# Two-head attention units on partition halves, without stacking transfers, in a gated attention and expert kernel

## The chip, the cores and the metric

One core of one Trainium2 chip. The metric is the device time of one execution in microseconds. The change is compared with the kernel before by medians of several runs.

## The reference

Two batches of 256 tokens of width 128 pass a gated attention and a gated mixture of experts; a context of 512 rows per batch gives further keys and values.

```
k = concat(LN(x) @ Wk1, ctx @ Wk2);  v = concat(LN(x) @ Wv1, ctx @ Wv2)   # 768 keys, 8 heads of 64
attn = softmax((LN(x) @ Wq1) k^T / 8);  x = x + tanh(g0) * ((attn v) @ Wo + bo)
combine = softmax of the top 2 of 8 of (LN(x) @ gate_w + gate_b)
out = x + tanh(g1) * (sum_e combine_e * ffn_e(LN(x)) + shared_ffn(LN(x)))  # gelu, hidden 512
```

Nine feed-forward networks (8 experts and the shared one) for two batches make 18 FFN steps.

## The kernel before

Precision comes from splitting each operand into an fp16 high part and an fp16 rest. ScalarE writes the high part, VectorE the rest out of PSUM (L720 for projections), and TensorE does three matmuls (hi hi, hi lo, lo hi; `three`, L904).

*Items.* `ITEMS` lists 27 projection outputs: transposed context `tc` and rows `tx`, keys `k` of a head pair (768 columns), queries `q`, values `v` of a key tile. Each passes TensorE, ScalarE (L589), VectorE (L720). The first 18 run ahead of attention, 9 are late items inside its steps. The weights are split by ScalarE and VectorE (L557, L692), and WV2 and WO by GpSimd (L501 to L505).

*Stacking.* A head has 64 rows. To fill 128 rows, SP's queue copies k and q, high parts and rests, from `k_nat` and `q_nat` into `kab` and `qab` (`stack_k`, `stack_q`, L404 to L425). These issues stand in one queue with the loads of the FFN weights (`load_f`, L388); the ring of FFN weights has 4 slots.

*Attention.* One step per head, 16 of them. `max_scores` (L987, L988) gives rough scores of 128 queries by 768 keys, VectorE takes their maximum (L735), a transpose (L1024) and L832 make of it a shift row. `scores` (L1006, L1007) is two matmuls per tile of 128 keys: 128 stacked rows, and 66 rows (rest and shift). ScalarE does the exponential (L598) and the fp16 copy (`make_hi`, L606) on 128x768, GpSimd the rest (`prob_lo`, L521), TensorE the product with v (`values`, L1041 to L1043), VectorE the division (L740, L745). The lags between these are 2, 3 and 4 steps. PSUM: banks 0 and 1 for maxima, 2 to 5 for scores, 6 for values, 7 for the rest.

*Tail.* When a batch's heads are done, stages run at fixed steps (`TAIL0`, `tail_of`): two transposes with a split (O0, O1), the product with Wo and row statistics (WO), normalised rows xn (X: power on GpSimd L538, VectorE L686, transpose L1065), router logits (GATE, exponential on GpSimd L542), the combination weights (COMB: VectorE L761 to L771, transpose L1076), bias (B2).

*FFN.* In FFN step k: h = W1 x (12 matmuls, L906 to L908), gelu (L642), fp16 cast on VectorE (L852), rest on GpSimd (L549), y = W2 h two steps later (24 matmuls of 128 columns), accumulation (L884). gelu(k) waits for the rest of step k-2. The weights of networks 0 to 2 are split by GpSimd ahead of attention (`split_early`, L489, L491, L493); those of 3 to 8 by ScalarE (L649) and VectorE (L892) in FFN steps 0 to 5. The first FFN step is step 18, so COMB of batch 0 (step 19) comes behind h(1).

The order on each engine is the program's: each engine runs through the steps and executes its parts of a step in the order written.

Of the kernel before, what the change touches and what calls it, by code (L numbers as in the profile page):

```python
# [14 lines left out]
F32 = mybir.dt.float32  # L15
F16 = mybir.dt.float16
# [4 lines left out]
P = 128  # L21
# [19 lines left out]
RING = 4  # L41
# [7 lines left out]
SHIFT_PAIR, = unpack("<f", pack("<ee", SHIFT_ROW, SHIFT_ROW))  # L49
# [6 lines left out]
ST_LAG = 2  # L56
HI_LAG = 3
PV_LAG = 4
FFN0 = NH + ST_LAG
# [3 lines left out]

TAIL0 = [HEADS + PV_LAG, NH + PV_LAG + 1]
BIAS_STEP = 10
EARLY = 3
FSPLIT0 = 15
# [4 lines left out]
def late_items(i, q):  # L72

    if i >= len(LATE_PLAN):
        return range(0)
    counts = [c for step in LATE_PLAN for c in step]
    n = NI - LATE + sum(counts[:2 * i + q])
    return range(n, n + counts[2 * i + q])


def place(h):

    return h % 2 * PAIRS + h // 2


def tail_of(i):

    return [(b, i - TAIL0[b]) for b in range(B) if i - TAIL0[b] in TAIL_STAGES]


def plan_items():

    items = [("tc", 0), ("tx", 0)]
    for p in range(PAIRS):
        items += [("k", 0, p), ("q", p)]
    items += [("v", 0, 0), ("tc", 1)]
    items += [("v", 0, t) for t in range(1, KT)]  # L100
    items += [("v", 1, t) for t in range(KT - LAST_V)]
    items += [("k", 1, p) for p in range(PAIRS)]
    items += [("v", 1, t) for t in range(KT - LAST_V, KT)]
    return items


LAST_V = 2
ITEMS = plan_items()
NI = len(ITEMS)
WARM_START, WARM_LAYERNORM, WARM_STEP = 14, 9, 8  # L110


LATE_PLAN = [(2, 2), (2, 1), (0, 1), (0, 1)]
LATE_SLOT = [1, 2, 3, 1, 2, 1, 2, 3, 3]
LATE = len(LATE_SLOT)

SLOT = [(n - (NI - LATE)) % 4 for n in range(NI - LATE)] + LATE_SLOT


def before(n, slot):  # L120

    return max([m + 1 for m in range(n) if SLOT[m] == slot], default=0)

SPLIT_BEFORE = {1: [WK2, WK1], 2: [WQ], 5: [WV2], 8: [WV1], 10: [WO]}
SPLIT_ORDER = [w for n in sorted(SPLIT_BEFORE) for w in SPLIT_BEFORE[n]]
# [5 lines left out]
GROUPS = [[(0, 1), (1, PAIRS)], [(0, 2), (2, PAIRS)]]  # L133


def group_of(b, p):

    return max(p0 for p0, _ in GROUPS[b] if p0 <= p)


LO_LAST = NH - 1


def lo_tiles(j):

    return 3 if j < LO_LAST else 0


def pool_lo(j, g):

    return 2 * j + g + 1 - max(0, j - LO_LAST + (g == 1)) if j >= 0 else 0
# [22 lines left out]
def shifts_before(n):  # L174

    return sum(1 for u, m in MISC.items() if m < n and u[0] == "shift")


def plan_misc():

    uses = []
    for i in range(STEPS):
        if 1 <= i <= NH:
            uses.append(("shift", i - 1))
        if i == BIAS_STEP:
            uses.append(("b1", 0))
        for b, s in tail_of(i):
            uses.append((s, b))
    return {u: n for n, u in enumerate(uses)}
# [5 lines left out]
def block_kernel(nc, x, ctx_in, g_xattn, g_ffn, Wq1, Wk1, Wv1, Wk2, Wv2, Wo, bo,  # L195
                 gate_w, gate_b, w1, b1, w2, b2, ws1, bs1, ws2, bs2, out):
    stack = ExitStack()
    with stack:
# [23 lines left out]
        kab = sb("kab", [P, 2, HEADS, KEYS], F16)  # L222
        k_a = kab[:, 0]
# [135 lines left out]
        def item_out(n):  # L359

            kind = ITEMS[n][0]
            return span(2 * SLOT[n], KEYS if kind == "k" else 512)
# [833 lines left out]
```

## Time and profile before

| | us |
|---|---|
| median of 3 runs (172.03 to 174.6) | 172.52 |
| profiled execution | 172.02 |
| its span, first to last instruction | 169.7 |
| PE / DVE / ACT / POOL busy | 139.7 / 131.2 / 109.6 / 126.8 |
| mean granted TensorE clock | 0.988 |

PE is TensorE, DVE VectorE, ACT ScalarE, POOL GpSimd. The time is read as the span plus the 2.3 us around it. Busy PE counts pipelined matmuls: one lasts 0.27 us and the next starts 0.11 us after it.

### The profile page before, as it was taken

Reading aid. Unit: us, or ns where it says so; the run is one execution under the profiler, and the core shown is the slowest. Engines: PE = TensorE matmul, PEld = TensorE weight load, DVE = VectorE, ACT = ScalarE, POOL = GpSimd, SP = SyncE. Lnnn points to the kernel's source line nnn. Section 1 sums busy time; section 2 is a strip of 40 time slices with the busy share of each in tenths; the row PEclk is TensorE's granted clock in tenths of the full one; section 3 lists DMA queues with packets and bytes.
Section 4 is the critical chain, followed back from the end, with each engine's and each line's share of the span. In section 5 each row is a group of like instructions: output and inputs, shape, how many; then the busy total and the mean of one; then the engine's idle time right before and its main releaser. Section 6 shows DMA issues by size and latency. Waiting matters only on the chain.

```text
span 169.7 us, 4332 instructions
## 1 busy us (share of the span) xinstructions
PE 139.7 (82%) x1724; PEld 111.5 (66%) x1724; DVE 131.2 (77%) x255; ACT 109.6 (65%) x182; POOL 126.8 (75%) x90
## 2 busy tenths in 40 slices
PE   7789588558699989999998892979866995999953
PEld 4435234335478768787787792869856994999952
DVE  1779999667667868768869689989999889454691
ACT  3369583329969979899968998569523462555600
POOL 7609999919999999989777955596557585868750
PEclk9999999999999999999999999999996999999999
DMA  4598699990004800995000000340000000100000
GB/s 136 184 315 211 196 238 242 220 251 14 6 0 85 198 1 16 217 233 191 4 4 0 4 0 0 108 144 6 2 0 0 4 0 4 31 0 4 0 0 31
DMA packets 12925, 13.99 MB, mean 82 GB/s; under 512 B 1470, under 2 KB 9579, under 8 KB 12907
## 3 DMA queue, kind: packets, MB, share of 16 engines
q1 hardware_dynamic: 12906, 13.73, 30.4%
q8 instruction: 13, 0.21, 0.6%
q14 instruction: 6, 0.04, 0.1%
HBM read 7.18 MB, written 0.26 MB: 44 GB/s over the span
## 4 chain that ended last, share of the span: by engine, by line
PE 32%; DVE 28%; POOL 10%; ACT 9%; DMA 8%; SPq 6%; issue 5%; DVEq 0%; ACTq 0%
PE banks L906 5%; DVE kab L852 5%; PE banks L908 5%; PE banks L907 5%; POOL kab L549 4%; ACT kab L642 4%; DVE v_lo L720 3%; DMA kab<-k_nat 3%; DVE nmax L735 3%; PE banks L1006 3%; PE banks L1007 3%; PE banks L987 3%; DMA ring<-in_L_ffn_w_dram 3%; SPq L425 2%; DVE gtop L763 2%
## 5 line engine op out<-in xcount | busy, mean ns | idle before, releaser
L549 POOL TENSOR_TENSOR kab<-kab 128x1024 f16<-128x1024 f32 (+1 forms) x18 | 41.1, 2283 | 17.3 <-DVE kab L852 17.3
L521 POOL TENSOR_TENSOR p_lo<-prob,p_hi 128x768 f16<-128x768 f32 x31 | 50.3, 1642 | 3.1 <-ACT p_hi L606 2.6
L642 ACT ACTIVATE kab<-banks,b1T 128x256 f32<-128x256 f32 x72 | 28.2, 478 | 24.3 <-PE banks L908 15.9
L735 DVE TENSOR_REDUCE nmax<-banks 128x1 f32<-128x768 f32 x32 | 30.5, 954 | 12.5 <-PE banks L988 12.5
L598 ACT ACTIVATE prob<-banks 128x768 f32<-128x768 f32 x32 | 25.8, 805 | 9.1 <-PE banks L1007 8.1
L906 PE MATMUL banks<-wf,kab 128*128 128x128 f16 x144 | 26.2, 224 | 5.8 <-POOL kab L549 4.5
L606 ACT ACTIVATE p_hi<-prob 128x768 f16<-128x768 f32 x32 | 27.0, 843 | 1.0
L852 DVE CAST kab<-kab 128x1024 f16<-128x1024 f32 (+1 forms) x19 | 19.5, 1031 | 9.8 <-ACT kab L642 9.8
L908 PE MATMUL banks<-wf,kab 128*128 128x128 f16 x144 | 26.2, 224 | 0.0
L907 PE MATMUL banks<-wf,kab 128*128 128x128 f16 x144 | 26.2, 224 | 0.0
L1006 PE MATMUL banks<-qab,kab 128*128 128x256 f16 x96 | 23.0, 273 | 0.7 <-DVE qab L832 0.7
L1007 PE MATMUL banks<-qab,kab 66*128 66x256 f16 x96 | 23.1, 273 | 0.0
L1041 PE MATMUL banks<-v_hi,p_hi 128*128 128x65 f16 x192 | 20.6, 194 | 2.0 <-POOL p_lo L521 2.0
L1043 PE MATMUL banks<-v_hi,p_lo 128*128 128x65 f16 x192 | 20.6, 194 | 0.0
L1042 PE MATMUL banks<-v_lo,p_hi 128*128 128x64 f16 x192 | 20.5, 193 | 0.0
L1041 PEld LDWEIGHTS banks<-v_hi,p_hi 128*128 128x128 f16 x192 | 17.8, 98 | 2.9 <-POOL p_lo L521 1.2
L906 PE MATMUL banks<-x2h,wf 128*128 128x256 f16 x72 | 19.6, 273 | 0.0
L908 PE MATMUL banks<-x2h,wf 128*128 128x256 f16 x72 | 19.6, 273 | 0.0
L907 PE MATMUL banks<-x2h,wf 128*128 128x256 f16 x72 | 19.6, 272 | 0.0
L906 PEld LDWEIGHTS banks<-wf,kab 128*128 128x128 f16 x144 | 14.5, 100 | 6.9 <-POOL kab L549 5.2
L1042 PEld LDWEIGHTS banks<-v_lo,p_hi 128*128 128x128 f16 x192 | 17.6, 98 | 0.3
L1043 PEld LDWEIGHTS banks<-v_hi,p_lo 128*128 128x128 f16 x192 | 17.6, 97 | 0.0
(144 smaller groups left out, 340.3 us busy)
## 6 DMA issues: line engine op xcount, KB each, us to landing
ring<-in_L_ffn_w_dram SPq DMA_DIRECT2D x16, 256.0 KB, 4.1
kab<-k_nat SPq DMA_DIRECT2D x4, 384.0 KB, 4.4
kab<-k_nat SPq DMA_DIRECT2D x6, 192.0 KB, 4.4
kab<-k_nat SPq DMA_DIRECT2D x2, 576.0 KB, 7.2
qab<-qo SPq DMA_DIRECT2D x2, 384.0 KB, 6.2
kab<-k_nat SPq DMA_DIRECT2D x2, 288.0 KB, 7.8
prob<-in_ctx_dram SPq DMA_DIRECT2D x2, 256.0 KB, 5.4
ring<-in_L_xattn_Wk_dram SPq DMA_DIRECT2D x2, 256.0 KB, 3.9
```

Of the source, the lines that this page charges most:

```text
L521: nc.gpsimd.tensor_tensor(p_lo[:, j % 3, dst, :], prob(j, g)[:, 0:n, :], p_hi[:, j % 3, dst, :], ALU.subtract).then_inc(pl_done, 1)
L549: nc.gpsimd.tensor_tensor(hid_lo[:, k % HB, cols], hid[:, k % 2, cols], hid_hi[:, k % HB, cols], ALU.subtract).then_inc(hl_done, 1)
L642: nc.scalar.activation(hid[:, k % 2, c * T1:(c + 1) * T1], span(2 * (k % 2), HC * T1)[:, c * T1:(c + 1) * T1], ACT.Gelu, bias=b1T[:, e * H ...
L735: nc.vector.tensor_reduce(nmax[:, i, q:q + 1], span(0, KEYS), AX_X, ALU.max, negate=True).then_inc(max_done, 1)
L906: nc.tensor.matmul(dst, w[0], a[0], start=start, stop=False)
L907: nc.tensor.matmul(dst, w[0], a[1], start=False, stop=False)
L908: return nc.tensor.matmul(dst, w[1], a[0], start=False, stop=stop)
L1006: nc.tensor.matmul(dst[:, cols], k_a[:, h, keys], q_a[:, h, queries], start=True, stop=False)
L1007: last = nc.tensor.matmul(dst[:, cols], k_b[0:DH + QT, h, keys], q_b[0:DH + QT, h, queries], start=False, stop=True)
L1041: nc.tensor.matmul(o_ps[:, q, :], ph, vh, start=(t == 0), stop=False, skip_group_check=True)
L1042: nc.tensor.matmul(o_ps[:, q, 0:DH], ph, vl, start=False, stop=False, skip_group_check=True)
L1043: last = nc.tensor.matmul(o_ps[:, q, :], pl, vh, start=False, stop=(t == KT - 1), skip_group_check=True)
```

## The change

The stacking copies and `kab`, `qab` go. k and q stay where the projections leave them: one head of a pair on partitions 0 to 63, the other on 64 to 127. Every attention matmul with k and q is done per half, the two halves alternating, into two PSUM banks. The unit of work is no longer one half of a head's keys but a pair of heads by two key tiles, 128x1024: 24 units (`NU`), three for each of 8 pairs, one per step. The shift row comes by a matmul of its own (ones row by shift) in both halves. Maxima are taken from the high parts alone (64 rows), in three chunks of 128x1024 per pair, four steps ahead. Score buffers: one (banks 2, 3) for units 0 to 8, then two. Four items stand ahead of the steps, the others at steps -4 to 7. The ring of FFN weights has 7 slots, so no load waits for stacking. On GpSimd only network 0 is split ahead of attention; networks 1 and 2, WO and the bias go between the units. The rest of the last unit is VectorE's. The 8 dummy matmuls in attention go. FFN is as before but starts at step 24 and keeps `hid` in the ring of exponentials; the first batch's tail starts at step 16, the second's at 27, so COMB of batch 0 (step 23) now stands before h(0).

```diff
-RING = 4
+RING = 7
-FFN0 = NH + ST_LAG
-TAIL0 = [HEADS + PV_LAG, NH + PV_LAG + 1]
+RINGP = 7
+RINGE = 3
+CHUNK0 = -(UPP + 1)
+DOUBLE0 = 9
+FFN0 = NU
+TAIL0 = [16, 27]
+def chunk_of(s):
+    p, c = divmod(s - CHUNK0, UPP)
+    return (p, c) if 0 <= p < NPAIR else None
+def shift_of(s):
+    p, r = divmod(s + 1, UPP)
+    return p if r == 0 and 0 <= p < NPAIR else None
+def values_of(s):
+    if s >= NU + 1:
+        return NH - 2 + s - (NU + 1) if s <= NU + 2 else None
+    p, r = divmod(s - (UPP + 2), UPP)
+    return 2 * p + r if p >= 0 and r < 2 and p < NPAIR - 1 else None
+PRE = [(("tc", 0), 0), (("tx", 0), 2), (("k", 0, 0), 4), (("q", 0), 6)]
+LATE = {
+    -4: [(("k", 0, 1), 2), (("q", 1), 7), (("k", 0, 2), 4), (("q", 2), 6)],
+    -3: [(("k", 0, 3), 2), (("q", 3), 7), (("v", 0, 0), 4), (("v", 0, 1), 5)],
+    -2: [(("v", 0, 2), 6), (("v", 0, 3), 7), (("v", 0, 4), 2), (("v", 0, 5), 3)],
+    -1: [(("tc", 1), 4), (("k", 1, 0), 6)],
+    0: [(("v", 1, 0), 4), (("v", 1, 1), 5)],
...
 # GpSimd
-            for j in range(1, EARLY):
-                if j == EARLY - 1:
-                    split_by_pool(WO)
-                split_early(j)
+            for i in range(STEPS):
+                if 0 <= i - 1 < LO_LAST:
+                    prob_lo(i - 1)
+                if i == 2:
+                    early_hi(1)
+                if i == 3:
+                    early_scaled(1)
+                if i == 4:
+                    early_lo(1)
+                if i == 5:
+                    add_bias()
+                if i == 6:
+                    early_hi(2)
+                if i == 7:
+                    early_scaled(2)
+                if i == 8:
+                    early_lo(2)
+                if i == 10:
+                    split_by_pool(WO)
 # ScalarE
+            def exp_unit(u):
+                act.wait_ge(score_ps, u + 1)
+                if u >= RINGE:
+                    act.wait_ge(pl_done, u - RINGE + 1)
...
+                if 0 <= i < NU:
+                    exp_unit(i)
+                for n in items[0:1]:
+                    item_of(n)
+                if 0 <= i < NU:
+                    make_hi(i)
+                for n in items[1:]:
+                    item_of(n)
...
+                    if k < 2:
+                        act.wait_ge(pl_done, NU - 2 + k)
 # VectorE
+            def part_max(p, c):
+                dve.wait_ge(max_ps, UPP * p + c + 1)
...
+                nc.vector.tensor_reduce(dst, src, AX_X, ALU.max).then_inc(part_done, 1)
 # TensorE
+            def scores(u):
+                p, third = divmod(u, UPP)
+                if score_before(u) > 0:
+                    pe.wait_ge(exp_done, score_before(u))
...
+                for n in range(KT2):
+                    for half in range(2):
+                        nc.tensor.matmul(dst[:, half, cols], k_of(p, half, 0, keys), q_of(p, half, 0, every), ...)
+                    for half in range(2):
+                        nc.tensor.matmul(dst[:, half, cols], k_of(p, half, 1, keys), q_of(p, half, 0, every), ...)
+                    for half in range(2):
+                        nc.tensor.matmul(dst[:, half, cols], k_of(p, half, 0, keys), q_of(p, half, 1, every), ...)
+                    for half in range(2):
+                        last = nc.tensor.matmul(dst[:, half, cols], ones_row[rows, :], shift[rows, p % 2, :], ...)
...
+            for i in range(CHUNK0, STEPS):
+                if shift_of(i) is not None:
+                    shift_row(shift_of(i))
+                if 0 <= i < NU:
+                    scores(i)
+                if chunk_of(i) is not None:
+                    max_chunk(*chunk_of(i))
                 k = i - FFN0
                 if 0 <= k < NF:
...
+                if values_of(i) is not None:
+                    values(values_of(i))
+                for n in late_items(i):
                     item_of(n)
...
                 for b, s in tail_of(i):
                     tail(b, s)
```

## Rows read from the trace of the kernel before

**Rows 1.** The page, busy time of each engine, its share, its instructions:
```profile
PE 139.7 (82%) x1724; PEld 111.5 (66%) x1724; DVE 131.2 (77%) x255; ACT 109.6 (65%) x182; POOL 126.8 (75%) x90
```

**Rows 2.** Attention stretch: busy PE, PEld, DVE, ACT, POOL (instructions), then clock, DMA share, GB/s:
```profile
48.00:76.00 28.00, 26.90 (x425) 21.83 (x423) 21.75 (x41) 24.92 (x31) 27.16 (x18) 1.00 0.48 111
```

**Rows 3.** Timeline of POOL ahead of attention: start, us, engine, line, tiles:
```profile
22.08 0.62 POOL L512 TENSOR_SCALAR bo_sb<-bo_sb,gates 128x128 f32<-128x128 f32 x1
22.78 1.69 POOL L515 TENSOR_TENSOR x_sb<-x_sb,bo_sb 128x128 f32<-128x128 f32 x4
24.43 1.89 POOL L489 TENSOR_TENSOR wf<-ring,c_sw 128x1024 f16<-128x1024 f32 x1
...
28.37 2.13 POOL L493 TENSOR_TENSOR wf<-ring,wf 128x1024 f16<-128x1024 f32 x1
30.45 1.04 POOL L501 TENSOR_TENSOR wa<-ring,c_sw 128x512 f16<-128x512 f32 x1
...
32.69 1.16 POOL L505 TENSOR_TENSOR wa<-ring,wa 128x512 f16<-128x512 f32 x1
37.72 1.89 POOL L489 TENSOR_TENSOR wf<-ring,c_sw 128x1024 f16<-128x1024 f32 x1 [3.88 <-DMA ring<-in_L_ffn_w_dram]
```

**Rows 4.** Timeline of POOL in attention:
```profile
43.76 29.41 POOL L521 TENSOR_TENSOR p_lo<-prob,p_hi 128x768 f16<-128x768 f32 x18
```

**Rows 5.** Timeline of DVE ahead of attention:
```profile
12.24 0.68 DVE L720 SCALAR_TENSOR_TENSOR qo<-banks,qo 128x512 f16<-128x512 f32 x1
...
20.73 3.76 DVE L720 SCALAR_TENSOR_TENSOR v_lo<-banks,v_hi 128x512 f16<-128x512 f32 x6
...
24.52 0.95 DVE L735 TENSOR_REDUCE nmax<-banks 128x1 f32<-128x768 f32 x1
```

**Rows 6.** Groups by line and shape: busy us, mean ns, idle before:
```profile
L735 DVE TENSOR_REDUCE nmax<-banks 128x1 f32<-128x768 f32 x32 | 30.5, 954 | 12.5 <-PE banks L988 12.5
...
L606 ACT ACTIVATE p_hi<-prob 128x768 f16<-128x768 f32 x32 | 27.0, 843 | 1.0
...
L598 ACT ACTIVATE prob<-banks 128x768 f32<-128x768 f32 x32 | 25.8, 805 | 9.1 <-PE banks L1007 8.1
```

**Rows 7.** Timeline of PE in attention:
```profile
60.67 0.27 PE L1006 MATMUL banks<-qab,kab 128*128 128x256 f16 x1
60.78 0.27 PE L1007 MATMUL banks<-qab,kab 66*128 66x256 f16 x1
...
61.12 0.19 PE L1041 MATMUL banks<-v_hi,p_hi 128*128 128x65 f16 x1
...
61.66 0.39 PE L987 MATMUL banks<-kab,qab 128*128 128x512 f16 x1
```

**Rows 8.** Timeline of POOL around the first batch's tail:
```profile
90.06 0.73 POOL L538 TENSOR_TENSOR rstd<-vare,c_mhalf 128x2 f32<-128x2 f32 x1 [1.25 <-DVE vare L679]
90.76 6.47 POOL L521 TENSOR_TENSOR p_lo<-prob,p_hi 128x768 f16<-128x768 f32 x4
...
102.68 2.12 POOL L549 TENSOR_TENSOR kab<-kab 128x1024 f16<-128x1024 f32 x1 [2.67 <-DVE kab L852]
```

**Rows 9.** Timeline of DVE around the first batch's tail:
```profile
91.72 2.36 DVE L686 TENSOR_SCALAR xn<-acc,mv,rstd 128x128 f32<-128x128 f32 x2
...
102.91 1.91 DVE L763 TENSOR_TENSOR gtop<-gtop,gexp 128x2 f32<-128x2 f32 x1
...
105.36 0.24 DVE L771 TENSOR_SCALAR comb_s<-comb,scales 128x18 f32<-128x18 f32 x1
```

**Rows 10.** Timeline of ACT in the FFN steps:
```profile
100.31 1.57 ACT L642 ACTIVATE kab<-banks,b1T 128x256 f32<-128x256 f32 x4
...
111.93 1.57 ACT L642 ACTIVATE kab<-banks,b1T 128x256 f32<-128x256 f32 x4 [2.55 <-POOL kab L549]
...
160.06 1.57 ACT L642 ACTIVATE kab<-banks,b1T 128x256 f32<-128x256 f32 x4 [1.08 <-PE banks L908]
```

**Rows 11.** Timeline of PE at the third FFN step:
```profile
105.74 0.38 PE L1076 MATMUL banks<-ident,comb 128*9 128x128 f32 x2 [3.04 <-DVE comb_s L771]
```

More of the change, by code:

```diff
@@ L9 @@
 from math import log
-from struct import pack, unpack
 import concourse.bass as bass
@@ L53 @@
 PICKED = 3.0e38
-ST_LAG = 2
-HI_LAG = 3
-PV_LAG = 4
-FFN0 = NH + ST_LAG
+KT2 = 2
+UPP = KT // KT2
+NPAIR = B * PAIRS
+NU = NPAIR * UPP
+RINGP = 7
[3 more added lines that the diff above has]
+FFN0 = NU
 NF = B * NE
 STEPS = FFN0 + NF + 4
-TAIL0 = [HEADS + PV_LAG, NH + PV_LAG + 1]
-BIAS_STEP = 10
+TAIL0 = [16, 27]
+BIAS_STEP = 12
 EARLY = 3
-FSPLIT0 = 15
+FSPLIT0 = FFN0 - EARLY
 TAIL_O0, TAIL_O1, TAIL_WO, TAIL_X, TAIL_GATE, TAIL_COMB, TAIL_B2 = TAIL_STAGES = (0, 1, 2, 4, 5, 7, 8)
[L72 to L78, printed above, removed]
@@ L81, in place @@
[L81 to L104, printed above, removed]
@@ L107, with tail_of @@
-LAST_V = 2
-ITEMS = plan_items()
-NI = len(ITEMS)
[L110 to L127, printed above, removed]
+def tail_of(s):
+    return [(b, s - TAIL0[b]) for b in range(B) if s - TAIL0[b] in TAIL_STAGES]
@@ new lines, with late_items, banks_of, before @@
+PLACED = PRE + [it for s in sorted(LATE) for it in LATE[s]]
+ITEMS = [it for it, _ in PLACED]
+BANK = [bank for _, bank in PLACED]
+NI = len(ITEMS)
+WARM_START, WARM_LAYERNORM = 14, 9
+def late_items(s):
+    n = len(PRE) + sum(len(LATE[r]) for r in LATE if r < s)
+    return list(range(n, n + len(LATE.get(s, []))))
+def banks_of(n):
+    return {BANK[n], BANK[n] + 1} if ITEMS[n][0] == "k" else {BANK[n]}
+def before(n, banks):
+    return max([m + 1 for m in range(n) if banks_of(m) & set(banks)], default=0)
@@ L171, in hid_parts @@
     return [(0, HC // 2), (HC // 2, HC)] if k in SHARED_LO else [(0, HC)]
-def shifts_before(n):
-    return sum(1 for u, m in MISC.items() if m < n and u[0] == "shift")
 def plan_misc():
     uses = []
[L182 to L185, printed above, removed]
+    for s in range(STEPS):
+        if s == BIAS_STEP:
             uses.append(("b1", 0))
-        for b, s in tail_of(i):
-            uses.append((s, b))
+        for b, t in tail_of(s):
+            uses.append((t, b))
     return {u: n for n, u in enumerate(uses)}
@@ L361, in item_out @@
             kind = ITEMS[n][0]
-            return span(2 * SLOT[n], KEYS if kind == "k" else 512)
+            return span(BANK[n], KEYS) if kind == "k" else banks[:, BANK[n], :]
         block = stack.enter_context(nc.Block())
@@ L991, in scores, with q_of @@
[L991 to L1002 removed]
+            def q_of(p, half, hl, cols):
+                b, pp = divmod(p, PAIRS)
+                return q_nat[DH * half:DH * half + DH, hl, b, pp, cols]
@@ new lines, in scores @@
+                    for half in range(2):
+                        nc.tensor.matmul(dst[:, half, cols], k_of(p, half, 1, keys), q_of(p, half, 0, every),
+                                         start=False, stop=False)
+                    for half in range(2):
+                        nc.tensor.matmul(dst[:, half, cols], k_of(p, half, 0, keys), q_of(p, half, 1, every),
+                                         start=False, stop=False)
+                    if u == 0 and n == 0:
+                        pe.wait_ge(consts, 5)
@@ L1009, in scores @@
+                    if third == 0 and n == 0:
+                        pe.wait_ge(shift_done, p + 1)
+                    for half in range(2):
+                        rows = slice(DH * half, DH * half + DH)
+                        last = nc.tensor.matmul(dst[:, half, cols], ones_row[rows, :], shift[rows, p % 2, :],
+                                                start=False, stop=True)
                 last.then_inc(score_ps, 1)
             def bank7_free(use):
-                n = MISC[use]
```

489 lines of the change are left out of this document (212 added, 277 removed), and 6 rows, old and new, of the table LATE.

## The prediction

> **What bounds the kernel now.** I read the busy times first. No engine is full over the span: PE 82%, DVE 77%, POOL 75% [rows 1]. So I read stretches. In attention, from 48 to 76 us, POOL works 27.2 of 28 us, PE 26.9 and ACT 24.9 [rows 2]. Three engines are about equal there. The reader should see that less work on one of them gains nothing unless the others follow.
>
> Then I read POOL alone, because it has no second engine to share with. Ahead of attention it waits 3.88 us for FFN weights whose load stood behind the stacking copies. It then splits network 2 from 37.72 on [rows 3], and its first p_lo starts at 43.76. Eighteen of them follow without a gap: 29.41 us, 1.634 us per 128x768 [rows 4]. The first gelu starts at 100.31 [rows 10], and 18 FFN steps and the end take the other 69.4 us. The steady distance of two gelus late in FFN is 1.57 + 1.08 = 2.65 us. Early steps take longer, 111.93 - 100.31 = 11.6 us for three [rows 10], mostly because PE waits for the router's combination weights of batch 0: they end at 105.36 + 0.24 = 105.6 [rows 9], after 3.04 us of PE waiting [rows 11].
>
> **What the change does to POOL.** p_lo becomes 23 pieces of 128x1024. The same kind of subtraction (f16 from f32 and f16) takes 2.12 us at that size [rows 8]; scaling 1.634 by 4/3 gives 2.18 [rows 4]. I take 2.12: 23 x 2.12 = 48.8 us, against 31 x 1.634 = 50.7 before. Work that stood ahead of attention now stands between units. The split of one network is 28.37 + 2.13 - 24.43 = 6.07 us, two are 12.1. The bias is 24.43 - 22.08, 2.4. WO is 32.69 + 1.16 - 30.45, 3.4 [rows 3]. Row powers and gate exponential are two short operations of 0.73, 1.5 [rows 8]. Sum: 48.8 + 12.1 + 2.4 + 3.4 + 1.5 = 68.2 us from the first p_lo to the last. Before, 17.9 us of this were done by 43.76, largely while POOL would otherwise have been idle; now POOL has nothing to do after network 0's split ends at 22.1.
>
> **When attention starts.** Stacking goes: no wait for DMAs, and FFN loads no longer stand behind them in SP's queue. The start now hangs on DVE. q of pair 0 is ready at 12.24 + 0.68 = 12.9; from there to 24.5 DVE ran 14 items and one weight split, 11.6 us [rows 5]. Two of these 14 (0.60 each, 3.76/6 by the row) now come later: 10.4. In between come three chunk maxima. At 768 columns one is 0.954 [rows 6], by size at most 1.27, and I take 1.2 because part is fixed: 3.6. The joining maximum and the shift add 0.7. Shift ready: 12.9 + 10.4 + 3.6 + 0.7 = 27.6. Then PE's chunk of pair 1 (0.45), its maximum 1.2, the context rest 0.6, k of batch 1 (1.0 by nine matmul slots of 0.11), scores 1.1: 31.95. The exponential of 128x1024 is 0.805 x 4/3 = 1.07 at most, the copy 0.843 x 4/3 = 1.12 [rows 6]; a v item of 0.6 stands between. First p_lo: about 34.5, with 32 to 36 as ends. That is 9 us earlier than now, and it is where the change earns.
>
> **POOL's chain.** Unit 1 is late by 1.2 us, since two v items and one k item stand on ACT before its copy. After that ACT needs 2.2 us per unit and its items, POOL 4.1 in steps 2 to 8, so POOL falls behind, up to the three buffers of exponentials. p_lo(18) ends at 34.5 + 1.2 + 19 x 2.12 + 12.1 + 2.4 + 3.4 = 93.9. The single score buffer costs nothing here: exponential, scores and latency are 2.4 us, and POOL's splits hide them up to unit 8. If POOL did not cover it, it would cost 9 x 0.3 = 3 us.
>
> **A new chain at the first batch's tail.** POOL's power comes behind p_lo(18): rstd at 94.6. Then DVE makes two xn tiles. In the trace these two, started at 91.72, took 2.36 us together, ending at 94.08 [rows 9], where POOL's second p_lo ended (90.76 + 2 x 1.62 = 94.0) [rows 8]. Such a DVE operation between SBUF tiles ends when POOL's running instruction does; the other case is 102.91 + 1.91 = 104.82 against 102.68 + 2.12 = 104.80 [rows 8, 9]. With units of 2.12 that gives xn at 94.6 + 4.2 = 98.8. PE waits for xn at the end of step 20, and behind it stand scores(21). Transposes 0.5, scores and latency 1.1, exponential 1.07, copy 1.12: p_lo(21) starts at 102.6, while POOL has been empty since 98.8. It ends at 104.7, the gate exponential at 105.4. p_lo(22) ends at 107.5, and L763 ends with it. The rest of the combination weights takes 105.6 - 104.8 = 0.8: ready at 108.3.
>
> **FFN after it.** Before, h(0) and h(1) ran ahead of COMB. Now COMB of batch 0 is in step 23 and PE, in order, waits for it before h(0). So all FFN steps start behind 108.3, gelu(0) at 109.6. DVE's list from there to the second cast: three normalisations (0.45 each), the last unit's rest 1.25, combT 0.4, bias 0.5, one weight split 1.2, two casts 0.7, and two waits for values, 0.9 and 1.1: 8.1. POOL's rest of step 1 is 2.1, so gelu(3) starts at 118.5 against 111.93 now [rows 10]. Behind gelu(3) both kernels have the same lists at the same distances: 57.8 us. Span 176.3, with the 2.3 us around it 178.6. That is 6.6 us over the profiled execution of 172.02 and 3.5% over the median 172.52.
>
> **TensorE.** Per pair, scores now are 48 matmuls of 64 rows and 256 columns. A matmul slot of 256 columns is 0.11 us, also where only 66 rows are used [rows 7]. If the two halves overlap fully, a unit is 8 slots, 0.88 us, and attention costs PE what it does now less half of the maxima, 5 us in all. If they don't overlap, it is 16 slots, 1.76. No row shows two disjoint halves. The 66-row row is the nearest, but it has a 128-row neighbour with which it could share nothing, so it doesn't decide; I take the lower end because each half has its own rows and its own PSUM bank, and keep both. With the lower end PE has 0.88 + 0.22 + 0.73 (values: 18 in 0.54 us, two thirds of 72) = 1.85 us per unit, below POOL's 2.12. The three matmuls of L906 to L908 are untouched.
>
> The Trainium skill, TensorEngine Tiling (Array Packing), section Tiling Modes, says that 64-row tiles work independently, but also that a change of tiling mode drains the array. By the first half of that PE stays at 1.85 per unit; by the second each step would pay for a change to 64 rows and one back. No row here shows what a drain costs.
>
> **Rivals.**
> *The halves don't overlap.* From unit 11 on PE then needs 1.76 + 0.3 + 0.73 = 2.8 us per unit, over POOL's 2.12. scores(11) can start at 69 (POOL's p_lo(8)), thirteen units and 3 us of tail end at 108.4, some 4.5 us later than in my chain; part was waiting anyway, leaving 3 us: 181.5. For it: nothing in the trace shows an overlap. Against: separate rows and banks. The change then doesn't do what its form is for.
> *No empty POOL at the tail.* If DVE gets its two xn in between POOL's units, POOL isn't starved (3.7 us back) and the router is ready earlier: 174.5, the same as before. For it: it needs only that POOL be less than a unit behind when the row powers are due, as now, where it waited 1.25 us for them [rows 8]. Against: POOL's sum, and the two rows named.
> *Faster: early FFN steps smooth.* The twelve first steps take 3.9 us each where 2.65 is steady [rows 10], an excess of 15 us, because DVE then carries the router of batch 0, weight splits and the second tail. The router's chain is now out of it, and values end before step 3. If each of these steps takes at most 3.1 us, 9.6 us come back: 169.0, and this decides faster. At the steady cadence it would be 164. Against: six weight splits and the second tail stay where they are relative to FFN.
>
> **How the numbers follow.** POOL and the tail chain as forecast: 0.50, 178.5, own range 175.5 to 181.5. No empty POOL: 0.18. No overlap: 0.17. Smooth FFN: 0.15. A measurement of this kernel tells about 2% from no change, so faster is below 169.1 and slower above 176.0. Faster 0.15; within 2% 0.27 (the second rival and the lower edge of the forecast); slower 0.58. Range 169 to 184: the unknown costs are start of attention (2 us each way), overlap (3 up), FFN pace.
>
> **What would show it.** p_lo(0) near 34.5, POOL's p_lo and splits without gaps from about 41 to 98, then a gap of some 4 us before p_lo(21). PE waiting for xn, then for the combination weights, and the first gelu at 108 to 110. Scores: 8 slots of 0.11 per unit. I am wrong if the last p_lo ends before 102, if gelu(3) comes before 114, or if a unit's 16 score matmuls take 1.76 us.

## The result, and the profile after

The changed kernel takes 187.63 us (median of 4 runs, 187.52 to 189.5) against 173.56 us for the kernel before in the same comparison. The ratio is 1.087, 95% interval 1.073 to 1.100: slower. I had forecast 178.5 us with a range of 169 to 184. The sign was right and the size was not: the loss was 14 us where I had 6, and the time lies outside the range. Some executions of either kernel are slower by a per cent or more whatever the program, and the ratios leave these out, so that a ratio can differ a little from the quotient of two medians.

The profiled execution took 187.71 us with a span of 185.9, which is 9.6 us over the 176.3 of my sum. First the busy times of the changed kernel (before: [rows 1]):

```profile
PE 145.1 (78%) x1900; PEld 109.4 (59%) x1900; DVE 130.5 (70%) x247; ACT 106.9 (57%) x166; POOL 119.9 (65%) x84
```

POOL, DVE and ACT have less to do than before, PE 5.4 us more, and the span is 16.2 us longer. So it is hardly work that was added; engines wait. Where they wait is read best from POOL, whose timeline I had forecast (start, us, engine, line, tiles, and in brackets the idle time just before with what ended it):

```profile
37.40 2.13 POOL L497 TENSOR_TENSOR p_lo<-prob,p_hi 128x1024 f16<-128x1024 f32 x1 [15.80 <-ACT p_hi L590]
40.53 2.13 POOL L497 TENSOR_TENSOR p_lo<-prob,p_hi 128x1024 f16<-128x1024 f32 x1 [1.01 <-ACT p_hi L590]
...
76.60 16.73 POOL L497 TENSOR_TENSOR p_lo<-prob,p_hi 128x1024 f16<-128x1024 f32 x8
94.18 2.13 POOL L497 TENSOR_TENSOR p_lo<-prob,p_hi 128x1024 f16<-128x1024 f32 x1 [0.85 <-ACT p_hi L590]
99.77 0.73 POOL L524 TENSOR_TENSOR rstd<-vare,c_mhalf 128x2 f32<-128x2 f32 x1 [3.46 <-DVE vare L660]
100.47 4.20 POOL L497 TENSOR_TENSOR p_lo<-prob,p_hi 128x1024 f16<-128x1024 f32 x2
109.61 2.12 POOL L497 TENSOR_TENSOR p_lo<-prob,p_hi 128x1024 f16<-128x1024 f32 x1 [4.94 <-ACT p_hi L590]
```

From 40.53 to 93.3 POOL has no gap, as forecast, and a unit takes 2.1 us. Then come the gaps: 3.46 us for the row statistics, which I had not foreseen, and 4.94 us for the next p_hi, where I had 3.8. In [rows 8] the wait for the statistics was 1.25 us. The timeline of DVE at the same place says why:

```profile
96.84 1.23 DVE L722 TENSOR_REDUCE part<-banks 128x4 f32<-128x1024 f32 x1 [2.41 <-PE banks L1001]
98.10 0.16 DVE L729 TENSOR_REDUCE nmax<-part 128x4 f32<-128x8 f32 x1
98.19 0.48 DVE L794 SCALAR_TENSOR_TENSOR acc<-banks,scales,x_sb 128x256 f32<-128x256 f32 x1
...
99.52 0.17 DVE L660 TENSOR_SCALAR vare<-mv 128x2 f32<-128x2 f32 x1
...
100.53 4.22 DVE L667 TENSOR_SCALAR xn<-acc,mv,rstd 128x128 f32<-128x128 f32 x2 [0.51 <-POOL rstd L524]
...
113.73 0.24 DVE L776 TENSOR_SCALAR comb_s<-comb,scales 128x18 f32<-128x18 f32 x1
```

The accumulation and the statistics (L794, L660) stand behind a chunk maximum that DVE first waits 2.41 us for. Then the two xn tiles take 4.22 us together, where [rows 9] has 2.36: they begin at 100.53, just behind the start of POOL's two p_lo at 100.47, and end with them (POOL at 104.67, DVE at 104.75).

PE pays for it (timeline of PE: two waits early; the last matmul of the product with Wo; the wait at the tail):

```profile
27.62 0.39 PE L996 MATMUL banks<-k_both,qo 64*128 64x512 f16 x2 [2.48 <-DVE shift L738]
30.10 0.59 PE L902 MATMUL banks<-cT,wa 128*128 128x512 f16 x1 [1.50 <-DVE cT L700]
...
95.38 0.22 PE L904 MATMUL banks<-wa,qo 128*128 128x128 f16 x1
...
104.90 0.66 PE L1098 MATMUL banks<-ident,xn 128*128 128x128 f32 x2 [4.08 <-DVE xn L667]
```

The product that L794 reads had left PE at 95.60, 2.6 us before L794 began. Behind both places the granted clock falls. This is the view by windows: length, then busy us and instructions of PE, PEld, DVE, ACT and POOL, and the PE clock as the third figure from the end:

```profile
26.00:28.00 2.00, 0.38 (x3) 0.19 (x4) 1.47 (x3) 0.00 (x0) 0.00 (x0) 1.00 0.00 0
28.00:30.00 2.00, 0.59 (x5) 0.36 (x4) 1.91 (x2) 0.60 (x1) 0.00 (x0) 0.68 0.00 0
30.00:32.00 2.00, 1.90 (x6) 0.74 (x6) 0.00 (x0) 0.00 (x0) 0.00 (x0) 0.50 0.00 0
...
104.00:106.00 2.00, 1.10 (x8) 0.68 (x10) 1.12 (x3) 0.38 (x1) 0.67 (x1) 0.50 0.03 8
...
112.00:114.00 2.00, 2.00 (x24) 1.23 (x21) 1.67 (x12) 1.83 (x2) 0.60 (x1) 0.50 0.00 0
```

PE was busy 0.97 us of the 4 between 26 and 30, and ran at 0.50, the lower of its two levels (1.2 GHz), until past 34. In 102 to 104 it did nothing, and from 104 to 114 it ran at 0.50 again. In these stretches PE's work takes twice its time: rows of scores start 0.21 us apart (105.68 and 105.89), elsewhere 0.11.

The first gelu starts at 117.56 instead of 100.31 [rows 10] or my 109.6 (timeline of ACT: what stands ahead of the first gelu, the first, the fourth):

```profile
112.13 1.02 ACT L582 ACTIVATE prob<-banks 128x1024 f32<-128x1024 f32 x1 [2.60 <-PE banks L1042]
...
116.27 1.28 ACT L623 ACT_TABLE_LOAD   x1
117.56 1.57 ACT L623 ACTIVATE prob<-banks,b1T 128x256 f32<-128x256 f32 x4
...
125.99 1.57 ACT L623 ACTIVATE prob<-banks,b1T 128x256 f32<-128x256 f32 x4 [1.11 <-POOL k_both L535]
```

I had PE waiting for the combination weights just ahead of it. That wait did not come. The weights were ready at 113.73 + 0.24 = 113.97, and PE reached their transpose later, with no idle time in front (PE timeline):

```profile
114.94 0.38 PE L1109 MATMUL banks<-ident,comb 128*9 128x128 f32 x2
```

ACT set the first gelu. From 112.13 on, when the scores of unit 22 let it go, it had no gap: two exponentials, two fp16 copies, a table load of 1.28 us, gelu.

From the first gelu to the end it is 185.9 - 117.56 = 68.3 us, against 69.4 before and 66.7 in my sum. So 17.3 us are lost before the first gelu, and the FFN gives 1.1 back: 16.2 us of span.

Last, the matmuls of the two halves (PE timeline):

```profile
81.68 0.28 PE L1028 MATMUL banks<-qo,k_both 64*128 64x256 f16 x2
81.80 0.27 PE L1031 MATMUL banks<-qo,k_both 64*128 64x256 f16 x2
...
82.57 0.38 PE L996 MATMUL banks<-k_both,qo 64*128 64x512 f16 x2
82.88 0.20 PE L1074 MATMUL banks<-v_hi,p_hi 128*128 128x65 f16 x1
```

Each row is two matmuls, one per half, and the rows are 0.11 us apart: from 81.68 to 82.57 a unit's 16 take 0.89 us, the slot of a single 256-column matmul per pair. The halves overlap.

### The profile page after: what moved, and what is told of

Same layout as the page of the kernel before. It is cut to its first block, busy times and chain, and to the rows that moved or that the text cites. A ratio compares the mean times of both kernels' runs of the same rounds, so it can differ in the third digit from the quotient of the medians.

```text
span 185.9 us, 4570 instructions
## 1 busy us (share of the span) xinstructions
PE 145.1 (78%) x1900; PEld 109.4 (59%) x1900; DVE 130.5 (70%) x247; ACT 106.9 (57%) x166; POOL 119.9 (65%) x84
## 4 chain that ended last, share of the span: by engine, by line
DVE 31%; PE 30%; POOL 21%; issue 8%; ACT 7%; DMA 2%; SPq 0%; DVEq 0%; ACTq 0%; POOLq 0%
POOL p_lo L497 12%; PE banks L902 6%; PE banks L903 6%; PE banks L904 5%; DVE k_both L850 5%; DVE wf L888 5%; DVE xn L667 4%; DVE part L722 3%; POOL wf L464 2%; POOL ring L459 2%; POOL wf L451 2%; DVE v_lo L700 2%; DVE wa L673 2%; DMA wf<-in_ctx_dram 2%; PE banks L1028 2%
## 5 line engine op out<-in xcount | busy, mean ns | idle before, releaser
L497 POOL TENSOR_TENSOR p_lo<-prob,p_hi 128x1024 f16<-128x1024 f32 x23 | 48.6, 2129 | 24.3 <-ACT p_hi L590 24.3
L535 POOL TENSOR_TENSOR k_both<-prob,k_both 128x1024 f16<-128x1024 f32 (+1 forms) x18 | 38.3, 2126 | 19.6 <-DVE k_both L850 19.6
L623 ACT ACTIVATE prob<-banks,b1T 128x256 f32<-128x256 f32 x72 | 28.3, 480 | 22.6 <-PE banks L904 14.5
L722 DVE TENSOR_REDUCE part<-banks 128x2 f32<-128x1024 f32 (+1 forms) x24 | 29.3, 1221 | 14.3 <-PE banks L996 9.7
L582 ACT ACTIVATE prob<-banks 128x1024 f32<-128x1024 f32 x24 | 24.5, 1022 | 17.9 <-PE banks L1042 12.6
L902 PE MATMUL banks<-wf,k_both 128*128 128x128 f16 x144 | 25.9, 223 | 5.3 <-POOL k_both L535 4.0
L904 PE MATMUL banks<-wf,k_both 128*128 128x128 f16 x144 | 25.9, 223 | 0.0
L903 PE MATMUL banks<-wf,k_both 128*128 128x128 f16 x144 | 25.9, 223 | 0.0
L590 ACT ACTIVATE p_hi<-prob 128x1024 f16<-128x1024 f32 x24 | 25.3, 1055 | 0.5
L850 DVE CAST k_both<-prob 128x1024 f16<-128x1024 f32 (+1 forms) x19 | 18.2, 960 | 9.5 <-ACT prob L623 9.5
L1028 PE MATMUL banks<-qo,k_both 64*128 64x256 f16 x96 | 14.7, 299 | 0.1
L1042 PE MATMUL banks<-shift,ones_row 64*128 64x256 f16 x96 | 14.6, 298 | 0.0
```

The source lines that it names most:

```text
L497: nc.gpsimd.tensor_tensor(p_lo[:, u % RINGP, :, :].rearrange("p a n -> p (a n)"), prob[:, u % RINGE, :], p_hi[:, u % RINGP, :, :].rearrang ...
L535: nc.gpsimd.tensor_tensor(hid_lo[:, k % HB, cols], hid[:, k % 2, cols], hid_hi[:, k % HB, cols], ALU.subtract).then_inc(hl_done, 1)
L590: nc.scalar.activation(p_hi[:, u % RINGP, :, :].rearrange("p a n -> p (a n)"), prob[:, u % RINGE, :], ACT.Copy).then_inc(ph_act, 1)
L623: nc.scalar.activation(hid[:, k % 2, c * T1:(c + 1) * T1], span(2 * (k % 2), HC * T1)[:, c * T1:(c + 1) * T1], ACT.Gelu, bias=b1T[:, e * H ...
L722: nc.vector.tensor_reduce(dst, src, AX_X, ALU.max).then_inc(part_done, 1)
L850: nc.vector.tensor_copy(hid_hi[:, k % HB, cols], hid[:, k % 2, cols]).then_inc(hh_done, 1)
```

## The experiments

The theory after the result: the loss is at the first batch's tail and the router, because the tail is placed where PE, DVE and POOL all go through it in order; POOL's splits between the units are hidden or cheap. Rivals: POOL's added work sets the time; the low clock does; the two halves cost more than one.

**All splits ahead.** Bias, network 1, WO and network 2 go ahead of the units on GpSimd; nothing else changes.

```diff
+            add_bias(); early_hi(1); early_scaled(1); early_lo(1)
+            split_by_pool(WO); early_hi(2); early_scaled(2); early_lo(2)
             for i in range(STEPS):
                 if 0 <= i - 1 < LO_LAST:
                     prob_lo(i - 1)
-                if i == 2: early_hi(1)
-                ...
-                if i == 10: split_by_pool(WO)
```

> GpSimd's bias, WO and the splits of networks 1 and 2 go ahead of the units, where it was idle from 21.6 to 37.4 us; nothing else is changed. Theory A (the work put between the units holds the attention up): this work is 17.9 us, so GpSimd is free for units from 39.5 on, 2 us later than now; units then go at the pace of ScalarE, about 2.4 us, p_lo(18) ends near 86 instead of 96.3, gelu(0) starts near 107 instead of 117.6, and the time is 176 to 179. Rival B (the chain at the first batch's tail sets the start of the FFN): the gap after p_lo(20) only grows, gelu(0) moves less than 3 us, time 185 or more.

Measured: 187.39 us (184.98 to 188.65), ratio 1.075 (1.066 to 1.085). By the medians that is 0.2 us less than the changed kernel, by the ratios 1%, for 17.9 us of work taken out from between the units. p_lo(18) ends at 91.98 instead of 96.31, and the first gelu is 3 us earlier. Theory A is out. The numbers of B came, but the gap ahead of p_lo(21) did not grow (4.93 us). The exponentials show what took over (ACT timeline, one pair of heads, three units):

```profile
60.35 1.02 ACT L574 ACTIVATE prob<-banks 128x1024 f32<-128x1024 f32 x1 [0.58 <-PE banks L1034]
62.73 1.02 ACT L574 ACTIVATE prob<-banks 128x1024 f32<-128x1024 f32 x1 [0.27 <-PE banks L1034]
65.13 1.02 ACT L574 ACTIVATE prob<-banks 128x1024 f32<-128x1024 f32 x1 [0.28 <-PE banks L1034]
68.17 1.02 ACT L574 ACTIVATE prob<-banks 128x1024 f32<-128x1024 f32 x1 [0.93 <-PE banks L1034]
```

A pair takes 68.17 - 60.35 = 7.8 us, and each time ACT waits for PE. POOL needs only 3 x 2.12 = 6.4, and the kernel before made a pair (four pieces) every 4 x 1.634 = 6.5 us [rows 4]. So GpSimd's list was not the one limit: right behind it stands a pace of the new attention that is slower than the old one. And the 3 us at the first gelu are 0.3 at the end of the span. From gelu(7) to gelu(9) it took 9.4 us instead of 7.6; the clock was 0.50 to 0.73 from 142 to 150 there, and 0.50 to 0.96 from 144 to 150 in the changed kernel. PE now also waited 2.96 us for the combination weights ahead of h(0).

**Dummy matmuls against the low clock.** 22 ahead of the first scores, 10 ahead of the second batch's first keys, 40 ahead of the transposed xn.

```diff
+                if i == -1:
+                    keep_warm(22, 5)
...
+                    if (b, p) == (1, 0):
+                        keep_warm(10, 5)
...
+                    if (s, b) == (TAIL_X, 0):
+                        keep_warm(40, 1)
```

> Dummy matmuls of 256 columns fill three idle stretches of TensorE: 22 before pair 1's chunk, 10 before the first keys of batch 1, 40 before it waits for xn. Theory C (the clock at 0.5 of full speed, granted at 29 to 36 and at 104 to 114 us after idle stretches, is a cost of its own): the clock stays 1.0 in both, p_lo(0) starts 1 us earlier, and the way from the end of xn to gelu(0), 12.9 us now, becomes 10.5 to 11; time 184.5 to 186. Rival (these stretches are bound by VectorE and GpSimd anyway): the clock stays up and the time is within 0.5 us of 187.6.

Measured: 186.7 us (186.31 to 188.41), ratio 1.078 (1.071 to 1.085); the mean clock rises from 0.935 to 0.971. The first p_lo starts at 35.15, 2.25 us earlier. (Three other runs without dummy matmuls, described below, have it at 36.13, 36.40 and 37.92, so the gain is 1.0 to 2.8 us.) Yet the first gelu gains only 1.7 us: from xn on, this kernel takes 13.4 us, more than the 12.9 of the changed one. PE, at clock 1.00, is through with the scores of unit 22 about 4 us after it got xn, instead of 7.2. But at the router two more small DVE operations are held:

```profile
106.43 2.12 DVE L815 TENSOR_TENSOR first<-logit,top 128x16 f32<-128x16 f32 x1
109.20 2.08 DVE L766 TENSOR_SCALAR gsum<-gexp 128x2 f32<-128x2 f32 x1
```

```profile
112.59 0.58 PE L1111 MATMUL banks<-ident,comb 128*9 128x128 f32 x2 [3.80 <-DVE comb_s L776]
```

In the changed kernel the same two take 0.16 and 0.17 us. Here POOL ran a p_lo from 106.36 to 108.51 and from 109.14 to 111.26, and the small operations end with it. So PE waits 3.80 us for the combination weights, and the clock falls again (0.58 and 0.56 in the windows 112 to 116). The low clock was a real cost, but behind it stood another one, the chain that I had forecast.

**xn on GpSimd.** The two xn tiles of each batch are computed by GpSimd right behind rstd.

```diff
-                if s == TAIL_X:
-                    normalise_rows(acc[:, tiles, :], NT + QT * b, QT, 2 + b)
+                        pool.wait_ge(rstd_ready, 2 + b)
+                        for q in range(QT):
+                            nc.gpsimd.tensor_scalar(xn[:, QT * b + q, :], acc[:, QT * b + q, :], ...)
```

> GpSimd makes the xn tiles of both tails itself, right behind the powers, in place of VectorE. Theory B (VectorE's xn is held until GpSimd's running instruction ends, twice): batch 0's xn, which took 4.22 us beside two p_lo, take two operations of about 0.6 us, xn is ready 2.7 us earlier, PE waits 1.4 instead of 4.1 us, p_lo(21) starts 3 us earlier, and the clock does not fall; time 183 to 185.5, as the second batch's xn (2.4 us) also leaves VectorE where it is full. Rival (the operations simply cost that much wherever they run): GpSimd's two take 2 us each and the time stays or grows.

Measured: 190.62 us (190.38 to 192.12), ratio 1.100 (1.094 to 1.107), slower than the changed kernel. The two tiles take 1.58 us there instead of 4.22 and POOL's gap ahead of p_lo(21) is gone, but the wait for the statistics stays at 3.45 us, and the first gelu comes only 1.1 us earlier. From there to the end it takes 73.8 us instead of 68.3. The second batch's xn (2.74 us) now stands in GpSimd's list, and at that place gelu(7) comes 8.1 us after gelu(6) instead of 6.0; the rest I can't put down to the edit, for the profiled execution took 192.12 us and the other three 190.4 to 190.8. My theory had POOL's gap as what matters. It was the chain to the combination weights: two operations of it took 2.17 and 2.09 us beside p_lo, and PE waited 4.3 us for its end.

**Halves in turn.** Four matmuls of one half, then four of the other, instead of alternating.

```diff
-                    for half in range(2):
-                        nc.tensor.matmul(dst[:, half, cols], k_of(p, half, 0, keys), q_of(p, half, 0, every), ...)
-                    for half in range(2): ...
+                    for half in range(2):
+                        (hi hi), (lo hi), (hi lo), (ones by shift), all of this half
```

> The same matmuls of the scores in another order: the four of one half, then the four of the other, per key tile. In the changed kernel two 64-row matmuls of different halves start together and 16 take 8 slots of 0.11 us. If only neighbours in the order overlap, 16 matmuls take about 14 slots, 1.5 us, one pair of neighbours in eight overlapping; units stay hidden under GpSimd's 4 us up to unit 8 and then cost 0.6 us more: time 189 to 195. If the engine overlaps halves whatever the order, a unit keeps 0.88 us and the time is 187.6 within 0.5.

Measured: 187.22 us (186.89 to 187.68), ratio 1.080 (1.074 to 1.086), within 0.4 us of the changed kernel. PE timeline:

```profile
83.18 0.29 PE L1033 MATMUL banks<-qo,k_both 64*128 64x256 f16 x2
83.30 0.28 PE L1035 MATMUL banks<-qo,k_both 64*128 64x256 f16 x2
83.41 0.28 PE L1037 MATMUL banks<-qo,k_both 64*128 64x256 f16 x2
...
84.06 0.40 PE L1001 MATMUL banks<-k_both,qo 64*128 64x256 f16 x4
```

The 16 matmuls still take 0.88 us, and those that run together were written four instructions apart. So the experiment did not take the overlap away, and can't price it. It shows that the order of the halves in the program doesn't matter here.

**First batch's tail two steps later.** COMB of batch 0 then stands behind h(0) and h(1), as before the change.

```diff
-TAIL0 = [16, 27]
+TAIL0 = [18, 27]
```

> The first batch's tail starts at step 18, not 16, so that COMB comes behind h(1), at step FFN0+1 as in the kernel before; nothing else. Theory B (COMB ahead of h(0), with xn's wait ahead of two units, puts the router's chain in line with the start of the FFN): units 19 to 22 are no longer behind the wait for the row statistics, gelu(0) starts at 110 to 112 instead of 117.6, and part is given back between gelu(1) and gelu(3), where PE waits for COMB as it did before; time 182 to 184.5. Rival (the wait only moves, the sum is the same): 187 to 188.5.

Measured: 181.54 us (179.93 to 182.32), ratio 1.057 (1.043 to 1.070). By the medians one constant gives 6.1 of the 14.1 us lost, by the ratios 5.2. The first gelu starts at 109.56, 8.0 us earlier; 1.3 of that was there at the first p_lo (36.13), where the constant has no part. PE waits 0.23 us for xn instead of 4.08, and 2.7 us for the combination weights behind h(1). The two xn take 0.6 us:

```profile
102.91 0.60 DVE L667 TENSOR_SCALAR xn<-acc,mv,rstd 128x128 f32<-128x128 f32 x2
```

POOL's next p_lo started at 103.48, when they were through. No other single edit that keeps the computation gained as much.

**Shift row behind the scores.** On top of the first experiment, PE issues the scores of a step ahead of the shift row.

```diff
-                if shift_of(i) is not None:
-                    shift_row(shift_of(i))
                 if 0 <= i < NU:
                     scores(i)
+                if shift_of(i) is not None:
+                    shift_row(shift_of(i))
```

> On the kernel with the splits ahead of attention: TensorE's shift-row transpose stands behind the scores of its step, not ahead of them. There units went at 2.63 us (7.9 per pair), two at 2.4 and one at 3.05, and TensorE stood 0.9 to 1.8 us per pair in front of the shift row, for the maximum of the chunk just ahead of it. Theory D (TensorE's own order sets the pace of attention once GpSimd is out of the way): the wait is covered by 0.88 us of scores, a pair takes 7.2, p_lo(18) ends at 87 instead of 92, gelu(0) 3 to 5 us earlier, time 182 to 184.5. Rival (ScalarE or the values' ping-pong with VectorE sets it): a pair stays at 7.9 and the time at 187.

Measured: 185.08 us (183.41 to 186.5), ratio 1.075 (1.059 to 1.091). The median is 2.3 us lower than that of the splits ahead, but against the kernel before the ratio is the same, so the gain is not shown by this. A pair still takes 7.7 us.

**The parts together.** First with network 2 left between the units, then with everything ahead; both with the later tail, the shift row behind the scores, and dummy matmuls (22 and 10).

> Together: bias, network 1 and WO ahead of the units (network 2 between them), the tail two steps later, the shift row behind the scores, and dummy matmuls in the two idle stretches before the first scores. If the costs found so far are separate: start -2.3, pace of attention -5, chain at the tail -4 on 187.6: 175 to 178. If they hide one another, 180 to 184.

> As the run before, but network 2 is split ahead of the units too, which holds p_lo(0) until 39.5 us and then leaves GpSimd 0.2 us per unit to spare. If TensorE's pace decides, it is within 1 us of that run; if GpSimd still decides there (23 units of 2.1 and 6 us from 36), this one is 1 to 3 us faster.

Measured: 178.64 us (176.14 to 179.35), ratio 1.034 (1.008 to 1.059), and 177.87 us (174.72 to 179.13), ratio 1.025 (1.000 to 1.050). The first lies just above its forecast, and the two are a tie. In the second the first gelu is at 105.10, and a pair still takes 7.7 us. Why, PE's timeline says (waits in one pair):

```profile
65.91 0.33 PE L1003 MATMUL banks<-ident,nmax 128*128 128x128 f32 x1 [0.65 <-DVE nmax L721]
66.84 0.39 PE L990 MATMUL banks<-k_both,qo 64*128 64x512 f16 x2 [0.61 <-DVE shift L730]
```

PE issues the last chunk, one unit's scores, and then waits for the maximum of that chunk, and again, with the next chunk, for the shift made from it, for both use banks 0 and 1.

**Values ahead of the chunk, and the price of the maxima.** In each third step: scores, shift row, values, chunk, with DVE in the same order; once with all splits ahead, once with network 2 between the units. The third kernel goes by the parts together, but leaves out the chunks, maxima and shift rows of pairs 1 to 7.

```diff
+                early_values = shift_of(i) is not None and values_of(i) is not None
+                if early_values:
+                    values(values_of(i))
                 if chunk_of(i) is not None:
                     max_chunk(*chunk_of(i))
...
-                if values_of(i) is not None:
+                if values_of(i) is not None and not early_values:
                     values(values_of(i))
```

> As e9 (all splits ahead, first tail two steps later, dummy matmuls, shift row behind the scores), and in each third step the order on TensorE is now scores, shift row, values, chunk, with VectorE in the same order. In e9 a pair of heads took 7.67 us: TensorE busy some 6.4, and 0.65 + 0.61 of waits, for the chunk's maximum (L721) and for the shift (L730). Theory A (this chain of maximum, transpose and shift sets the pace of attention): the second wait goes behind the values, the pair falls to about 7.05 us, seven pairs give 4 us, the first gelu comes at 101 to 102 and the time is 173 to 174.5. Rival B (another limit lies just behind, GpSimd with 6.3 us per pair and its latencies, or VectorE's order): the pair stays over 7.4 us and the time over 176.

> As e10, with the split of network 2 between the units of GpSimd as in e8 instead of ahead of them. e8 and e9 differed by 0.8 us. Theory A: once TensorE's pace is faster, GpSimd is the tighter engine, so the 6 us of network 2 weigh more between the units: 174 to 177, slower than e10. Rival B: attention starts earlier by as much and it is a tie with e10, within 1 us.

> As e9, but the chunks, maxima and shift rows of pairs 1 to 7 are left out, and all pairs use the shift of pair 0 (this part of the computation is changed). It prices the whole chain of maxima. Theory A: a pair is then bound by GpSimd, 6.4 us (three units of 2.12), against 7.67: 8 to 9 us less in attention, first gelu at 96 to 98, time 168 to 171. Rival B (the mixed order of scores and values on TensorE, not the maxima, sets the pace): the pair stays over 7.2 us and the time over 174.

Measured: 175.72 us (173.81 to 176.88), ratio 1.011 (0.994 to 1.027); 175.12 us (174.58 to 177.09), ratio 1.013 (0.999 to 1.027); 170.19 us (169.47 to 171.88), ratio 0.986 (0.969 to 1.002). The first two are a tie, and neither is shown to differ from the kernel before. The pair fell to 7.4 to 7.5 us, not to 7.05: the 0.61 went, but this one came (PE, network 2 between):

```profile
72.16 0.33 PE L1010 MATMUL banks<-ident,nmax 128*128 128x128 f32 x1 [0.65 <-DVE nmax L724]
73.50 0.39 PE L997 MATMUL banks<-k_both,qo 64*128 64x512 f16 x2
73.72 0.27 PE L1029 MATMUL banks<-qo,k_both 64*128 64x256 f16 x2
...
75.29 0.39 PE L997 MATMUL banks<-k_both,qo 64*128 64x512 f16 x2 [0.53 <-DVE part L717]
```

The chunk moved back by a block of values and so came closer to the next one, which waits until its maximum has left the same two banks. Without the maxima the exponentials follow each other like this (ACT timeline):

```profile
68.33 1.01 ACT L574 ACTIVATE prob<-banks 128x1024 f32<-128x1024 f32 x1
69.37 1.06 ACT L582 ACTIVATE p_hi<-prob 128x1024 f16<-128x1024 f32 x1
70.33 1.01 ACT L574 ACTIVATE prob<-banks 128x1024 f32<-128x1024 f32 x1
```

A unit takes ACT 2.00 us, exactly its two operations, and a pair 6.0. ACT can run ahead only by the three buffers of exponentials; behind it POOL has no gap (POOL timeline):

```profile
60.32 29.45 POOL L497 TENSOR_TENSOR p_lo<-prob,p_hi 128x1024 f16<-128x1024 f32 x14 [0.21 <-ACT p_hi L582]
```

Fourteen in 29.45 us are 2.10 each, so the pace that lasts is POOL's 6.3 us per pair, as theory A had it. The maxima through two banks make 7.4 to 7.9 of it. Their price in the time is 7.7 us by the medians (177.87 to 170.19) and 6.9 by the ratios, and it holds also the PE and DVE work that was left out.

**Rests of the tail ahead of the maxima.** On top of the kernel with values ahead of the chunk and network 2 between the units. There PE still waited 2.13 and 1.19 us for the rests of the first batch's transposed outputs, which stood behind a chunk maximum on DVE.

```diff
+                for b, s in tail_of(i - 1):
+                    if i < NU and s in (TAIL_O0, TAIL_O1):
+                        tail(b, s)
                 if shift_of(i) is not None:
                     shift_out(shift_of(i))
```

> As e11, and on VectorE the rest (L750) of the first batch's two transposed outputs (stages O0 and O1) stands ahead of the chunk maximum and the shift of its step, not behind them. In e11 TensorE waits 2.13 us for the first of them and 1.19 us for the second. Theory A (small steps of the tail that stand behind chunk maxima hold TensorE's order, the same cause as the late row statistics of the changed kernel): both waits go, 2 to 3.3 us less, and the time is 172 to 173.3, level with the kernel before. Rival B (TensorE waits just as long for the score buffers or for ScalarE there): less than 1 us, time 174.3 to 175.3.

Measured over 12 runs: 171.84 us (169.73 to 175.34) against 173.37, ratio 0.990 (0.985 to 0.997). The two waits fell to 0.3 us in all. The first gelu starts at 98.50, 1.8 us before that of [rows 10]; the FFN takes 70.3 us, 0.9 more than before. DVE and POOL at the tail now:

```profile
91.94 0.60 DVE L662 TENSOR_SCALAR xn<-acc,mv,rstd 128x128 f32<-128x128 f32 x2
```

```profile
88.93 2.13 POOL L497 TENSOR_TENSOR p_lo<-prob,p_hi 128x1024 f16<-128x1024 f32 x1 [0.34 <-ACT p_hi L585]
91.17 0.73 POOL L519 TENSOR_TENSOR rstd<-vare,c_mhalf 128x2 f32<-128x2 f32 x1
92.43 4.31 POOL L497 TENSOR_TENSOR p_lo<-prob,p_hi 128x1024 f16<-128x1024 f32 x2 [0.53 <-ACT p_hi L585]
```

POOL waits 0.53 us between rstd and its next p_lo, and the two xn fit in. By the medians this version takes 8% less than the changed kernel. Against the kernel before it is 1% less, by an interval that just leaves out 1, which is level by the 2% that the forecast asked for. So the form with two halves did not itself cost the 14 us. It was where its parts stand in the order, and for a part that was not singled out the low clock, since this version keeps the dummy matmuls.

## Why the prediction was right and wrong

**Right.** Slower, and in the place named: the first batch's tail, in order on PE, holds the first FFN step. Of the two waits that I named there, the one for xn came (4.08 us) and the one for the router's weights did not; it shows only in versions where PE is faster (2.96 and 3.80 us). POOL's units take 2.1 us, its list has no gap to 93.3, the halves overlap (that rival, 0.17, is refuted), xn takes two of POOL's units (4.22 us, forecast 4.2), and gelu(3) comes 8.4 us after gelu(0), forecast 8.9. The smooth early FFN steps (rival, 0.15) did not come: the twelve first take 3.8 us each, against 3.9 before. That POOL needn't be empty at the tail (rival, 0.18) was wrong in a way that teaches: its condition was met, as POOL waited for the statistics, and POOL was emptied all the same. The p_hi of its next p_lo had been there since 98.74, so that this p_lo began the moment rstd ended, ahead of DVE's xn. In the later versions it wasn't ready, and xn took 0.6. None of the three signs of being wrong that I had written down came: I had looked for errors that make the kernel faster and for the overlap, not for a late input.

**Wrong.** The sum was 9.6 us short of the span, term by term:

- The start. I took 34.5 for the first p_lo, with 36 as the far end; it was 37.40, 2.9 us late. The shift was ready at 27.6, to the tenth where I had it (PE's row at 27.62), but I costed PE's work behind it at the full clock. PE, idle for 2.48 and 1.50 us, ran it at 0.50. With the dummy matmuls it was 2.25 us less than that, and 1.0 to 2.8 us less than in the other runs without them.
- POOL's chain gave 0.5 back, so p_lo(18) ended 2.4 us late, at 96.31.
- "POOL's power comes behind p_lo(18)". The step that failed most. I let rstd follow POOL's own list and never asked when its input was ready. On DVE the statistics stand behind a chunk maximum, and POOL waits 3.46 us. With the 2.4 us, xn ends at 104.7 instead of 98.8.
- xn to gelu(0) was 12.9 us instead of 10.8. The weights came 9.3 us after xn, where I had 9.5, but nothing waited for them. At 0.50, PE took 7.2 us from xn to the scores of unit 22, and behind them ACT had two units (4.1 us) and the table load of 1.28 us, which has no term in my sum. With the clock up the weights decide, and this stretch was no shorter (13.4 us). All this makes 8.0 us at gelu(0).
- Behind it 1.6 us more: 0.5 less than forecast up to gelu(3), and 59.9 instead of 57.8 from there. I took the lists and distances behind gelu(3) to be those of before. But gelu(5) comes 7.8 us after gelu(3), not 5.9. DVE has no gap there, and two of its weight splits ran beside POOL's rests (DVE timeline; the same two took 1.20 and 2.12 us before):

```profile
124.07 2.97 DVE L888 SCALAR_TENSOR_TENSOR wf<-ring,wf 128x1024 f16<-128x1024 f32 x1
...
128.08 2.85 DVE L888 SCALAR_TENSOR_TENSOR wf<-ring,wf 128x1024 f16<-128x1024 f32 x1
```

The "1.85 us per unit" of PE, below POOL's 2.12, was a sum of busy time with no waits in it (its terms add up to 1.83). Up to unit 17 it did no harm to the forecast, because POOL's splits were slower still; but it is why the first experiment gave so little, and by it I took the wrong view of what the change could earn. With the splits ahead PE's pace was 2.6 us a unit: 2.38 us in a step with values (scores 0.89, chunk 0.31, values 1.1, and gaps) and 3.05 in the third, for the maxima.

The Trainium skill, TensorEngine Tiling (Array Packing), section Tiling Modes, says that 64-row tiles work independently, which the trace bears out. Its drain at a change of mode is small here: from the chunk (82.57) to the values (82.88) it is 0.31 us, against 0.22 from such a chunk to the next scores (73.50 to 73.72 above). That is 0.09 us more per change, about 0.2 us per unit.

What stays open: how the 5 to 6 us of the later tail divide between COMB behind h(1) and xn in 0.6 us, for both came with the one constant (the waits speak for xn and the statistics, as PE did not wait for the weights before the move); how much of the last version's time the dummy matmuls and the shift row behind the scores give, for they were not taken out of it singly; and whether the chain of maxima could be taken out of PE's order with the same eight banks. The last was not tried.

## What to carry to other kernels

Ask for every small step of a chain (statistics, a rest, a power) what stands ahead of it in its engine's program order, and when its input is ready; here the biggest costs were matters of placement, not of work. Where several engines carry nearly equal loads, a sum of busy times per unit is a lower bound and no pace: follow one loop through the buffers it reuses, and count its latencies. And cost work on TensorE that follows an idle stretch at the lower clock as well as the full one.

## What the runs showed of the hardware

- Matmuls of the two 64-row halves overlap also when four of one half are written ahead of four of the other: 16 in 0.88 us either way.
- Small DVE operations between SBUF tiles often end when POOL's running one does: two xn took 4.22 us with POOL busy and 0.60 without; the router's L815 and L766 took 2.12 and 2.08 us beside a p_lo, and 0.16 and 0.17 in the changed kernel. Not all are held: two MAX8 of the router took 0.24 us beside a p_lo (changed kernel, 110.52).
- Between 26 and 30 PE was busy for 0.97 us; the granted clock fell to 0.50 there and stayed so until past 34. Between 102 and 104 PE did nothing, and the clock was 0.50 from 104 to 114, though PE was busy without a break from 106 on.
- Between matmuls on 64 and on 128 rows some 0.09 us go by beyond the usual distance, as said above.
